# Finished tokens of the last mixture: 32 indirect stores issued by GpSimd in place of eight plain stores issued by SyncE

## The reference, cut to what matters

```python
x2 = _layernorm(src, ln2_g, ln2_b)
sel = jax.nn.sigmoid(x2 @ sel_w)
scores, idx = jax.lax.top_k(sel, K)                     # K = 4 of E = 32 experts
gate = (jax.nn.one_hot(idx, E, dtype=sel.dtype) * scores[..., None]).sum(-2)
h = jax.nn.relu(jnp.einsum('bsd,edh->bseh', x2, keys))  # 128 -> 128 for every expert
moe_out = jnp.einsum('bseh,ehd,bse->bsd', h, values, gate)
return src + moe_out
```

## Time and profile before

| what | value |
|---|---|
| time, median of 3 runs (lowest to highest) | 3017.76 us (3016.76 to 3022.34) |
| span of the profiled execution, first to last instruction | 3012.5 us |
| PE busy over the span | 2830.3 us, 94% |
| POOL busy over the span | 2034.0 us, 68% |
| POOL busy from 2700 to 2800 us, inside f6m | 93.17 of 100 us |
| mean granted TensorE clock over the span | 0.974 |
| the last mixture, first matmul to end of span | 2630.8 to 3012.5 us |

### The profile page before, as it was taken

One profiled execution on the slowest core, in us unless ns is written; L12 is line 12 of the kernel. 1 busy time (PEld: TensorE's weight loads), 2 busy tenths in 40 slices (PEclk: granted clock), 3 DMA queues, 4 the chain that ended last, 5 costly groups with the idle time before them and its releaser, 6 DMA issues. The chain is left out here.

```text
span 3012.5 us, 62032 instructions
## 1 busy us (share of the span) xinstructions
PE 2830.3 (94%) x21152; PEld 2279.5 (76%) x21152; DVE 1969.1 (65%) x4330; ACT 1853.5 (62%) x5061; POOL 2034.0 (68%) x2542
## 2 busy tenths in 40 slices
PE   7999797899879999998999989998999999999999
PEld 5888575688768888886788856665888888768887
DVE  6554587545458888886555556774888888755554
ACT  2333353333279999996444446776999999754444
POOL 4323674323168888876999974555888888689998
PEclk9999899999989999999999989998999999999999
DMA  3000564000022222223555555552222221255554
GB/s 109 6 1 1 115 141 99 1 1 1 9 64 44 43 44 61 47 58 113 183 185 184 196 158 116 113 103 47 44 47 60 44 44 43 56 205 194 194 193 165
DMA packets 152507, 266.07 MB, mean 88 GB/s; under 512 B 14099, under 2 KB 124947, under 8 KB 129139
## 3 DMA queue, kind: packets, MB, share of 16 engines
q1 hardware_dynamic: 152194, 262.11, 31.1%
HBM read 204.06 MB, written 53.67 MB: 86 GB/s over the span
## 5 line engine op out<-in xcount | busy, mean ns | idle before, releaser
L3139 POOL TENSOR_TENSOR f4m_ht_lo<-f4m_ht,f4m_ht_hi 128x512 fp32r<-128x512 f32 x256 | 331.5, 1311 | 38.6 <-ACT f4m_ht_hi L3064 28.0
L3139 POOL TENSOR_TENSOR f6m_ht_lo<-f6m_ht,f6m_ht_hi 128x512 fp32r<-128x512 f32 x256 | 331.2, 1307 | 32.3 <-ACT f6m_ht_hi L3064 19.8
L3109 DVE SCALAR_TENSOR_TENSOR f6m_ht<-f6m_hr,f6m_gate 128x512 f32<-128x512 f32 x256 | 176.4, 691 | 167.8 <-PE f6m_hr L2986 101.8
L3109 DVE SCALAR_TENSOR_TENSOR f4m_ht<-f4m_hr,f4m_gate 128x512 f32<-128x512 f32 x256 | 175.8, 690 | 162.9 <-PE f4m_hr L2986 94.7
L3064 ACT ACTIVATE f4m_ht_hi<-f4m_ht 128x512 fp32r<-128x512 f32 x256 | 161.6, 632 | 193.8 <-DVE f4m_ht L3109 193.6
L3064 ACT ACTIVATE f6m_ht_hi<-f6m_ht 128x512 fp32r<-128x512 f32 x256 | 161.7, 632 | 191.1 <-DVE f6m_ht L3109 190.9
L2660 ACT ACTIVATE f4a_pr<-f4a_sr,f4a_nm 128x256 f32<-128x256 f32 x512 | 243.1, 495 | 23.6 <-DVE f4a_nm L2728 23.2
L2660 ACT ACTIVATE f6a_pr<-f6a_sr,f6a_nm 128x256 f32<-128x256 f32 x512 | 243.0, 495 | 21.4 <-DVE f6a_nm L2728 20.9
L2814 POOL TENSOR_TENSOR f4a_rr<-f4a_tmp 128x256 f32<-128x256 f32 x256 | 186.7, 730 | 92.1 <-DVE f4a_tmp L2736 90.5
L2814 POOL TENSOR_TENSOR f6a_rr<-f6a_tmp 128x256 f32<-128x256 f32 x256 | 186.8, 730 | 83.6 <-DVE f6a_tmp L2736 81.8
L2736 DVE TENSOR_TENSOR f4a_tmp<-f4a_ur,f4a_turn 128x512 f32<-128x512 f32 x256 | 175.3, 685 | 60.9 <-PE f4a_ur L2525 57.1
(11 more groups left out here) (582 smaller groups left out, 9399.6 us busy)
## 6 DMA issues: line engine op xcount, KB each, us to landing
f4m_gate<-f4o_gates SPq DMA_DIRECT2D x64, 1024.0 KB, 4.7
f6m_gate<-f6o_gates SPq DMA_DIRECT2D x64, 1024.0 KB, 4.7
r_scratch<-r_parts SPq DMA_DIRECT2D x32, 192.0 KB, 2.3
all_qs<-r_scratch SPq DMA_DIRECT2D x16, 384.0 KB, 4.9
all_ks<-r_scratch SPq DMA_DIRECT2D x16, 384.0 KB, 6.8
f4al_scratch<-f4a_parts SPq DMA_DIRECT2D x32, 192.0 KB, 2.2
all_qs<-f4al_scratch SPq DMA_DIRECT2D x16, 384.0 KB, 5.0
all_ks<-f4al_scratch SPq DMA_DIRECT2D x16, 384.0 KB, 6.7
```

Of the source, the lines that this page charges most:

```text
L3109: nc.vector.scalar_tensor_tensor(ht[:, n % RB, :], hr[:, n % HB, :], 0.0, gate[:, q % GB, n % LOADED, :], ALU.max, ALU.mult).then_inc(ht_r ...
L3139: nc.gpsimd.tensor_tensor(ht_lo[:, n % RB, :], ht[:, n % RB, :], ht_hi[:, n % RB, :], ALU.subtract)\
```

## The change

In the second mixture SP no longer stores tokens. POOL makes a table `rows` once (row n of a tile in partition p is 128 n + p, an iota of 128 x 32), and issues for each group four indirect DMAs, one per tile, each writing 128 rows of 512 bytes to the rows that a column of the table names. For groups 0 to 6 they stand in POOL's list at e = 10 of the following group, between the ht_lo of expert 9 and of expert 10; for the last group at the end. The order in POOL's list is fixed: what stands behind them waits until POOL has issued them.

```diff
-        stored = a.sem("stored")
+        stored, rows_ready = a.sem("stored"), a.sem("rows_ready")
+        rows = a.sb("rows", [P, G * GT], U32)
...
-            def store_tokens(g):
-                sp.wait_ge(x_done, g + 1)
-                sp.dma_start(out.rearrange("b (t p) c -> p (b t) c", p=P)[:, g * GT:(g + 1) * GT, :],
-                             x_sb[:, g * GT:(g + 1) * GT, :]).then_inc(stored, 16)
...
-                if out is not None and q % (E1 // LOADED) == E1 // LOADED - 1 and q >= E1 // LOADED:
-                    store_tokens(q // (E1 // LOADED) - 1)
...
             if out is not None:
-                store_tokens(G - 1)
-                sp.wait_ge(stored, 16 * G)
+                sp.wait_ge(stored, 16 * G * GT)
...
+            def store_tokens(g):
+                pool.wait_ge(x_done, g + 1)
+                for n in range(g * GT, (g + 1) * GT):
+                    nc.gpsimd.indirect_dma_start(out.rearrange("b t c -> (b t) c"),
+                                                 bass.IndirectOffsetOnAxis(ap=rows[:, n:n + 1], axis=0),
+                                                 x_sb[:, n, :], None).then_inc(stored, 16)
+
+            if out is not None:
+                nc.gpsimd.iota(rows[:, :], pattern=[[P, G * GT]], base=0, channel_multiplier=1).then_inc(rows_ready, 1)
             opening.root(pool, LATE)
             for n in range(N):
                 g, e = n // E1, n % E1
+                if out is not None and e == 10 and g:
+                    if g == 1:
+                        pool.wait_ge(rows_ready, 1)
+                    store_tokens(g - 1)
                 pool.wait_ge(hi_ready, n + 1)
...
+            if out is not None:
+                store_tokens(G - 1)
```

## The result

| | median of the runs (lowest to highest) |
|---|---|
| before | 3017.26 us (3015.82 to 3022.34), 4 runs |
| changed | 3060.68 us (3058.01 to 3065.70), 4 runs |

The ratio is 1.014, with a 95% interval from 1.0128 to 1.0153: the change costs 43 us, and the interval reaches from 38.6 to 46.2. The forecast was 3056, 38 more than before.

What follows compares the result with a forecast made beforehand. PE was taken to set the pace, with POOL second and hardly any room. Stalls and end, 32d - 7.8 = 32 us at d = 1.25, plus 6 us for the clock made 38, on 3017.8: 3056 us, range 3024 to 3100.

Steps and rivals of the forecast that it cites:

- What bounds the kernel: In f6m, PE is busy throughout a 45 us window, POOL for 42.07; POOL can catch up nearly 4 us a group.
- d = 1.25 us: Time one indirect DMA holds POOL, put nearest to one pass over a 128x512 tile; likely ends 0.71 and 2.34.
- longer first use: Sign of being wrong: POOL holds something else up, such as a first use that takes longer; no size given.
- The stall at e = 10: Groups 1 to 7: PE waits for POOL's lateness beyond a 1.5 us cushion, 3.36 us each, 23.5 us in all.
- x_lo: At e = 14 in groups 1 to 6, POOL's low part of x stalls PE 0.69 us each, 4.1 us in all.
- The clock: Granted clock falls behind half of the seven stalls or a little less, 3 x 2 = 6 us.
- The end: After the last addition, POOL issues four DMAs, the last landing some 1.9 us behind; 4d - 0.4 = 4.6 us.
- The base: Median of the runs taken 5.3 us above the profiled span of 3012.5, giving 3017.8 us before the 38 added.
- Cheap issue: Rival: d under 0.41 us on POOL, only the end pays 0.4 to 1.2 us, 3018 to 3019; chance 0.08.
- not on the path: Rival: POOL's other instructions run beside the DMA issue; no measurable change, 3018 to 3019; chance within a shared 0.08.
- Faster: Rival: SP's shorter list frees gate loads, or a smaller last store lands sooner; 3017, over 6 us needed; chance 0.01.
- Row by row: Rival: issue on POOL far dearer, d over 2.34; at 6.92, 214 us, or 228 with seven clock drops, 3246; chance 0.09.

Runs made afterwards that it cites:

- spread kernel: Against the changed kernel, a group's four indirect DMAs stand one each at e = 10, 17, 22 and 27; 3039.42 us, ratio 1.0072.
- half-size DMA: Against the changed kernel, each of the 32 indirect DMAs writes only 64 rows, half of the output left out; 3055.87 us, ratio 1.0131.
- later-placed kernel: Against the changed kernel, the four indirect DMAs in a row stand at e = 24 in place of e = 10; 3058.94 us, ratio 1.0136.
- paired kernels: Against the changed kernel, a group's four indirect DMAs stand two at e = 10 and two at e = 22; 3044.18 us, ratio 1.0080.

## Why the prediction was right, step by step

**What bounds the kernel.** PE sets the pace, POOL has hardly any room: held. One more number would have helped. The room of a group is 45 us less 41.3, which I called nearly 4 us; 1.5 of them are pauses and longer steps that POOL cannot fill. For the burst this made no difference, for the spread kernel it made the missing 0.6 us a group. And one row was misread: the prediction takes DVE's row as a wait for POOL because the bracket names ht_lo. By the prediction's own count the ht_lo that it needs had ended 1.4 us before; what it needs and what ended at that moment is PE's third matmul into hr:

```profile
2735.43 0.40 PE L2986 MATMUL f6m_hr<-f6o_x_hi,f6o_keys_lo 128*128 128x512 f32 x1
```

It ends at 2735.83 and DVE starts at 2735.87. That DVE did not wait for gates there, which is what the sum needs, is true either way.

**d = 1.25 us.** 1.26 to 1.27 measured (0.96 and a gap of 0.30). That the value was met so closely is luck. It was taken by likeness to a pass over a tile, and that likeness was no mechanism: half of the rows cost 1.20. What was sound is the sum that d goes into, and the range of 0.71 to 2.34. The first DMA of the program takes 1.24 us in place of 0.96. It costs group 1 0.3 us (a stall of 3.44 where the other odd groups have 3.16). The prediction had named a longer first use among the signs of being wrong; it came, and is this small.

Two pages of the Trainium skill stood beside d. The page DMA: Bandwidth & Descriptors (Specifications) gives about 1 us to the first byte on the path from GpSimd; POOL is held for 1.26 us and the earliest landing is 2.2 us after the issue, so neither number here is that latency, and no run shows the first byte. The page GPSIMD Engine Reference (Performance pitfalls for Q7 kernels) gives 102 cycles to each small read, from which 10.9 us a DMA were estimated. The half-size DMA doesn't agree: 1 ns a row. What reads the table here is not priced that way.

**The stall at e = 10, forecast 3.36 x 7 = 23.5 us.** PE's idle times are 3.44, 3.05, 3.16, 3.06, 3.16, 3.05 and 3.16, together 22.1 us. To each belongs about 0.3 us that no idle time shows. The matmul that waited lasts 0.50 for 0.39, and the next step is 1.50 us for 1.39: in the later-placed kernel an idle time of 3.12 makes the group 3.39 longer. So the step costs 22.1 + 7 x 0.3 = 24.2 us.

**x_lo, forecast 0.69 x 6 = 4.1 us.** The stall is 0.35 to 0.39 us of idle time where it comes, and 0.64 with the after-effect: the two steps in group 1 are 1.87 and 1.49 us for 1.36. It came in groups 1, 3 and 5 and was gone in 2, 4 and 6, where PE had been slow; that saving the forecast had put into the term of the clock. On the same terms it is 6 x 0.64 = 3.8 us.

**The clock, forecast 3 falls x 2 = 6 us.** In the profiled execution there were four. What one costs is best read from two executions of the same loop, the changed kernel and the one that only differs at the end. Group 1 takes 49.16 us without a fall and 50.08 with one; group 3 48.86 and 49.79; group 4 49.08 and 50.05; group 5 48.90 and 49.76. That is 0.9 us a fall, net of the x_lo stall that it spares. The forecast's 2 was over-sized for these because the slow stretch is about 3.4 us and not 6: the 6 were read at a place where PE kept idling. But longer ones occur without that. In group 6 of the kernel that differs at the end the stretch lasted 5.7 us and the group took 51.19, 2.1 more than the 49.08 of group 4 with a held clock: that is the forecast's 2. In group 7, with no x_lo and a slow stretch of 5.7 us, the fall costs 2.6 (the group and the rest up to the last addition are 6.1 us longer, less 3.16 + 0.3 for the stall). So 3 x 0.9 + 2.6 = 5.3 us: more falls than forecast, three of the four cheaper. That the product came out near 6 is luck.

Together 24.2 + 3.8 + 5.3 = 33.3 us, which is what the loop has; the forecast had 33.6. The terms were read from this loop, so that they add up to it is bookkeeping; what tests them are the other kernels.

Whether the clock falls is not decided by the length of the stall alone: behind 3.44 us it held in the changed kernel, behind 3.05 us it fell. Over the four kernels with bursts it fell behind 2 of 6 stalls of 2.8 to 2.9 us, 12 of 17 of 3.05 to 3.2, and 4 of 5 of 3.4 to 3.7. After the stalls of at most 1.4 us of the spread and the paired kernels it never fell. The Trainium skill (TensorE: Matmul & The Clock Gate) has the clock fall after an idle stretch; the prediction took from it that a longer stall makes the fall surer. These counts lean that way and are too few to show it, and all seven in one execution did not come. What decides in the single case stays open.

**The end, forecast 4.6 us.** Measured 5.2; the kernel that changes the end alone 6.3 by its medians (its interval is 2.7 to 8.4). Its trace has 10.3 us from the last addition to the end, +4.9, although its first indirect DMA is the longer one of 1.24 us: the program ended 3.6 us behind the last DMA, in the changed kernel 4.8 behind it. So what follows the last DMA varies by as much as the forecast missed.

**The base.** The forecast put the median 5.3 us above the span. The profiled execution of the changed kernel has a time of its own, 3058.76 for a span of 3056.8: 2.0 us lie around the span. If as much lies around the span of before, that execution took some 3014.5 us, and the other 3.3 us mean that it was a quick one. As the sum was added to the median, this did not move the forecast.

**The difference of the medians.** Loop and end of the two traces explain 38.5 us of 43.4. The profiled execution had four falls of the clock; the kernel with the same loop had six and a loop of 341.5 us (2706.65 to 3048.10), +36.2. With the end's 5.2 this is 41.4. The rest, 2 us, is less than the interval of the ratio (38.6 to 46.2). That the typical execution has more falls than the profiled one is an inference from two traces, not shown.

**The rivals.** Cheap issue and "not on the path": out, since POOL stands for 4.95 us. Faster: out; the kernels with plain DMAs from GpSimd have SP's shorter list too, and the quickest of them is 1.2 us slower than before. Row by row: out by the half-size DMA.

## What to carry to other kernels

A DMA that GpSimd issues is work of GpSimd: look at what that engine does at that place and how late it may be, not at the bytes. Count the DMAs (here 1.26 us each if indirect and in a row, 1.17 if alone, 0.54 to 0.77 if plain), compare what stands in a row with the cushion in time, and the whole with the room of the loop less the pauses that it cannot use. If the row numbers are regular, a plain DMA of a whole group from an engine that has nothing else to do was the quickest of all that were measured here; if it has to be GpSimd, few large ones, or small ones spread out.

## What the runs showed of the hardware that was not expected

- An indirect DMA of 64 rows costs GpSimd 1.20 us, one of 128 rows 1.265: half of the rows save 5% of it. Plain ones cost 0.54 us (128 rows) and 0.77 (512 rows), so 384 more rows, 0.6 ns each.
- Behind an indirect DMA GpSimd has a gap of 0.30 us before the next one that counts as issue; four plain ones follow each other without it, 2.15 us for four.
- The first indirect DMA of a program takes 1.24 us against 0.96, the first plain one from GpSimd 0.80 against 0.54.
- Here a matmul that waited for its operand costs about 0.3 us more than the idle time that the profile puts down to the wait.
- Of seven stalls of 2.8 to 3.7 us the granted clock fell behind four in the changed kernel, six with the same loop and another end, six with the later place, and two with half the rows. The same stall of the same loop brought a fall in one execution and none in another, and the slow stretch behind it lasted from 3 to 5.7 us.
